# Cross attention over a long context: the key/value projection in pairs of 16-bit floats and 32-column matmuls

## The reference, cut to what matters

```python
q = x @ Wq.T                                   # x is layer-normalised
k_raw, v_raw = context @ Wk.T, context @ Wv.T
kv = concatenate([k_raw, v_raw], -1).reshape(b, m, 32, 8, 2)
k, v = kv[..., 0], kv[..., 1]                  # per head
q, k = rmsnorm(q), rmsnorm(k)                  # eps 1e-6
attn = softmax(q k^T * 8 ** -0.5)              # over 2048 context rows
x = x + attn @ v
```

## Time and profile before

| | before |
|---|---|
| median of 3 runs | 417.14 us (415.88 to 417.5) |
| span of the profiled execution | 413.8 us |
| PE busy | 388.5 us, 94% of the span |
| DVE, ACT, POOL busy | 303.8, 267.0, 208.3 us |
| L1790 matmuls (projection) | 192, busy 53.0 us |
| L1833 matmuls (values), L1820 (scores) | busy 69.7 and 25.9 us |
| L1741 (exponentials) | 128, busy 123.8 us |

### The profile page before, as it was taken

One profiled execution on the slowest core, in us unless ns is written; L12 is line 12 of the kernel. 1 busy time (PEld: TensorE's weight loads), 2 busy tenths in 40 slices (PEclk: granted clock), 3 DMA queues, 4 the chain that ended last, 5 costly groups with the idle time before them and its releaser, 6 DMA issues.

```text
span 413.8 us, 14357 instructions
## 1 busy us (share of the span) xinstructions
PE 388.5 (94%) x5999; PEld 322.5 (78%) x5999; DVE 303.8 (73%) x693; ACT 267.0 (65%) x553; POOL 208.3 (50%) x257
## 2 busy tenths in 40 slices
PE   6889989999999999889999999999889989999996
PEld 4567766777677777669999897778778878989995
DVE  7787989998688888758999996787997768222220
ACT  3588878887888888986454533823999136444441
POOL 2566677666566665106644440610498634445530
PEclk9999999999999999999999999999999999999999
DMA  5637731642321110380000017120000590000000
GB/s 162 230 117 245 232 123 52 195 141 73 85 65 39 30 29 6 114 320 2 2 2 1 2 44 306 39 103 2 2 0 3 176 388 2 2 1 2 0 2 25
DMA packets 10832, 34.78 MB, mean 84 GB/s; under 512 B 2192, under 2 KB 7312, under 8 KB 8976
## 3 DMA queue, kind: packets, MB, share of 16 engines
q1 hardware_dynamic: 10624, 33.86, 23.9%
q10 hardware_dynamic: 144, 0.00, 0.0%
HBM read 33.60 MB, written 0.26 MB: 82 GB/s over the span
## 4 chain that ended last, share of the span: by engine, by line
PE 59%; DVE 18%; POOL 9%; issue 8%; ACT 3%; DMA 1%; SPq 0%; DVEq 0%; POOLq 0%; ACTq 0%
PE ps L1833 10%; PE ps L1790 8%; PE ps L1244 8%; PE ps L1226 6%; PE ps L1820 4%; PE ps L1803 3%; PE ps L956 3%; PE ps L938 3%; PE ps L454 2%; PE ps L897 2%; POOL sb_halves L1632 2%; ACT sb_arena L1741 2%; PE ps L904 2%; DVE sb_big L635 2%; PE ps L1214 1%
## 5 line engine op out<-in xcount | busy, mean ns | idle before, releaser
L1741 ACT ACTIVATE sb_arena<-ps 128x1024 f32<-128x1024 f32 x128 | 123.8, 1020 | 19.2 <-PE ps L1820 18.3
L1833 PE MATMUL ps<-sb_arena 128*25 128x128 f32 (+1 forms) x2048 | 69.7, 274 | 1.9 <-issue 1.3
L1833 PEld LDWEIGHTS ps<-sb_arena 128*25 128x25 f32 (+1 forms) x2048 | 50.4, 97 | 10.0 <-issue 1.8
L1790 PE MATMUL ps<-sb_halves 128*128 128x512 f32 x192 | 53.0, 411 | 3.4 <-POOL sb_halves L1632 2.5
L1282 POOL TENSOR_TENSOR sb_halves<-sb_big,sb_halves 128x704 fp32r<-128x704 f32 x19 | 32.1, 1689 | 38.4 <-ACT sb_halves L1274 38.4
L1790 PEld LDWEIGHTS ps<-sb_halves 128*128 128x128 f32 x192 | 33.5, 188 | 16.0 <-issue 6.0
L1392 DVE SCALAR_TENSOR_TENSOR sb_arena<-ps,sb_w_q,sb_arena 128x176 f32<-128x176 f32 x40 | 15.9, 401 | 40.3 <-ACT sb_arena L1300 40.0
L1244 PE MATMUL ps<-sb_halves 128*128 128x352 f32 x240 | 43.7, 333 | 1.8 <-DVE sb_halves L1345 1.0
L544 POOL TENSOR_TENSOR sb_halves<-sb_big,sb_halves 128x256 fp32r<-128x256 f32 x28 | 21.6, 793 | 44.3 <-ACT sb_halves L528 44.3
L1623 POOL TENSOR_TENSOR sb_big<-sb_arena 128x256 f32<-128x256 f32 x30 | 18.7, 624 | 47.0 <-DVE sb_arena L1500 47.0
L1244 PEld LDWEIGHTS ps<-sb_halves 128*128 128x128 f32 x240 | 39.0, 189 | 3.6 <-issue 2.4
(11 more groups left out here) (249 smaller groups left out, 850.6 us busy)
## 6 DMA issues: line engine op xcount, KB each, us to landing
sb_arena<-in_ctx SPq DMA_DIRECT2D x32, 128.0 KB, 2.8
sb_mid<-in_w_down SPq DMA_DIRECT2D x1, 3584.0 KB, 11.7
sb_big<-in_w_gu SPq DMA_DIRECT2D x1, 3520.0 KB, 11.8
sb_mid<-in_w_ffn SPq DMA_DIRECT2D x3, 768.0 KB, 4.5
sb_big<-in_w_gu SPq DMA_DIRECT2D x1, 2112.0 KB, 8.0
sb_big<-in_w_q SPq DMA_DIRECT2D x2, 1024.0 KB, 5.1
sb_big<-in_w_k SPq DMA_DIRECT2D x2, 1024.0 KB, 6.3
sb_big<-in_w_v SPq DMA_DIRECT2D x2, 1024.0 KB, 5.7
```

What stands on the lines that cost most here:

```text
L1741: nc.scalar.activation(probs[:, n % P_SLOTS].rearrange("p a g n -> p a (g n)"), ps[:, bank:bank + 2], ACT.Exp, scale=XD ** -0.5).then_inc( ...
L1790: i = T.matmul(ps[:, 7], ctx_half[:, t % 2, c, kt], wkv_half[:, d, kt], start=(n + kt == 0), stop=(n == 2 and kt == KT - 1))
L1833: i = T.matmul(ps[32 * gg:32 * gg + m, 6, j * P:(j + 1) * P], v_sb[:, t % V_SLOTS, 4 * gg + j, head], probs[:, n % P_SLOTS, a, gg], start= ...
```

## The change

Context and weights are still split into a high and a low part, but the parts are 16-bit floats (F16). The key/value weights are multiplied by 256 when they are split (on ScalarE by an activation with a scale in place of a copy, on VectorE by a scalar_tensor_tensor in place of a tensor_tensor); the ones that count the softmax's denominator become 256, and the epsilon of the keys' norm is multiplied by 256 squared. The pairs lie in a part of `w_ri` that is not yet loaded then, no longer in `halves`. In `project`, each of the six matmuls of 128 columns becomes four of 32 columns that write 32 partitions each of the same bank, 24 in all. The order of the steps on every engine and all waits stay as they are; the lines of the kernel below L1552 move down by one to four (the matmul L1790 becomes L1794).

```diff
-        wkv_half = halves[:, 0:2048].rearrange("p (c k n) -> p c k n", c=2, k=KT)
-        ctx_half = halves[:, 2048:3072].rearrange("p (s c k m) -> p s c k m", s=2, c=2, k=KT)
+        x_pairs = w_ri[:].rearrange("p c t n -> p (c t n)")
+        wkv_half = x_pairs[:, 1024:2048].bitcast(F16).rearrange("p (c k n) -> p c k n", c=2, k=KT)
+        ctx_half = x_pairs[:, 2048:2560].bitcast(F16).rearrange("p (s c k m) -> p s c k m", s=2, c=2, k=KT)
...
-            V.memset(v_sb[:, :, :, 8:9], 1.0)
-            V.memset(v_sb[:, :, :, 33:34], 1.0)
+            V.memset(v_sb[:, :, :, 8:9], W_SCALE)
+            V.memset(v_sb[:, :, :, 33:34], W_SCALE)
...
-            V.tensor_tensor(wkv_half[:, 1], w_xkv, wkv_half[:, 0].bitcast(F32), ALU.subtract).then_inc(sem("wkv_split"), 1)
+            V.scalar_tensor_tensor(wkv_half[:, 1], w_xkv, W_SCALE, wkv_half[:, 0], ALU.mult, ALU.subtract
+                                   ).then_inc(sem("wkv_split"), 1)
...
-                G.tensor_tensor(ctx_half[:, t % 2, 1], ctxT[:, t % CTX_SLOTS], ctx_half[:, t % 2, 0].bitcast(F32),
+                G.tensor_tensor(ctx_half[:, t % 2, 1], ctxT[:, t % CTX_SLOTS], ctx_half[:, t % 2, 0],
                                 ALU.subtract).then_inc(sem("ctx_split"), 1)
...
-            nc.scalar.copy(wkv_half[:, 0], w_xkv).then_inc(sem("wkv_high"), 1)
+            nc.scalar.activation(wkv_half[:, 0], w_xkv, ACT.Copy, scale=W_SCALE).then_inc(sem("wkv_high"), 1)
...
-                nc.scalar.activation(kln, kms[:, t % 2], ACT.Ln, bias=1e-6, scale=1.0 / XD).then_inc(sem("k_log"), 1)
+                nc.scalar.activation(kln, kms[:, t % 2], ACT.Ln, bias=1e-6 * W_SCALE ** 2, scale=1.0 / XD).then_inc(sem("k_log"), 1)
...
                     for kt in range(KT):
-                        i = T.matmul(ps[:, 7], ctx_half[:, t % 2, c, kt], wkv_half[:, d, kt], start=(n + kt == 0),
-                                     stop=(n == 2 and kt == KT - 1))
+                        for r in range(0, P, 32):
+                            i = T.matmul(ps[r:r + 32, 7], ctx_half[:, t % 2, c, kt, r:r + 32], wkv_half[:, d, kt],
+                                         start=(n + kt == 0), stop=(n == 2 and kt == KT - 1), skip_group_check=True)
```

More of the change, by code:

```diff
@@ L52 @@
 TURN_AT = 13
+W_SCALE = 256.0
 LATE_GU = slice(4 * 2 * EI, E * 2 * EI)
```

## The result

After the change the kernel takes 425.7 us (median of 4 runs, 422.9 to 428.3) against 417.3 before: a ratio of 1.021, 95% interval 1.018 to 1.024. I had forecast 414.0 and a range up to 416.8. It is slower, by 8.4 us, where I had forecast some 3 less.

What follows compares the result with a forecast made beforehand. VectorE and GpSimd's loop (4.69 to 4.81 us) was taken to bind, practically tied with TensorE's 4.71. Gains of 0.8 + 0.3 + 0.8 + 0.8 + 0.4 = 3.1 off the span of 413.8, plus 3.3, gave 414.0 us, range 409.5 to 416.8.

Steps and rivals of the forecast that it cites:

- The projection: Key/value projection on TensorE: 24 matmuls of 32 columns take 1.49 us instead of 1.66, 0.17 less a round.
- the early switch: On TensorE, from values to projection: the projection starts 0.18 before the values' end instead of 0.07, 0.11 less a round.
- TensorE's own round: Cross attention, one projection to the next on TensorE: from 4.71 to 4.43 us, 0.28 less.
- less overlap: Rival on the projection's four column groups: 0.28 a group, 24 matmuls in 1.79, no gain, 416.5 to 417.5 us; chance 0.13.
- two pairs: Rival on the projection: only two column groups run at a time, projection 2.6 us, kernel 439 us; chance 0.04.
- The loop of VectorE and GpSimd: Cross attention: the two engines wait on each other in a closed loop, 4.69 us a round, 4.81 in the first half.
- GpSimd's split: Context split on GpSimd, now writing 16 bits: no change taken, bounds -0.1 and +0.08 us a round.
- TensorE really binds: Rival in the cross attention: TensorE sets the round, so its whole saving counts, 8.2 us, 408.9 us; chance 0.10.
- rounds of 4.4: Sign in the cross attention: rounds falling to 4.4 us would prove the prediction wrong, TensorE binding after all.
- More halts for instructions: Rival on TensorE's queue: one more halt of 1.11 us gives 415.1, three 417; chance 0.08, shared with a slower cast.
- The single stretches of the sum: Gains by part of the cross attention: 0.8 + 0.3 + 0.8 + 0.8 + 0.4 = 3.1 us off the span.
- The frame: Step from profiled span to measured time: the median lies 3.3 us above the span, 410.7 becoming 414.0.

Runs made afterwards that it cites:

- e1_wide: The changed kernel with the projection as six 16-bit matmuls of 128 columns instead of 24 of 32: 412.6 us, 0.990 of the kernel before.
- e9_light_pool: e1_wide with GpSimd's two weighing steps on 8 columns instead of 128, most of the weighted sum left out: 414.5 us, 0.997 of the kernel before.
- e4_wide_turn: The changed kernel with keys turned by 8 transposes of 128 columns instead of 32 of 32: 410.4 us, 0.985 of the kernel before.
- e5_held_loads: The changed kernel with later parts' weights loaded together after the last context tile: time not compared; last values end at 179.0 us, 11.7 earlier.
- e2_waits: The kernel before the change with 1152 already fulfilled waits added to TensorE's queue: 460.8 us, 1.103 of the kernel before.

## Why the prediction was wrong

**The projection: right.** The 24 matmuls take 1.48 against 1.49, the early switch is 0.18, and TensorE's own round is 4.41 against 4.43. The rivals with less overlap and with two pairs, at 1.79 and 2.6, are out. The Trainium skill, "TensorE: Matmul & The Clock Gate", section "Measured speedup vs the span model", gives 3.07 times for four row tiles with 512 moved. Carried over to four column groups, as the prediction did, that meant an estimated 0.29 a group; the trace does not agree, with 24 matmuls in 1.48.

**The loop of VectorE and GpSimd: right, and a little shorter.** Where no halts disturb it, the second half goes at 4.62 and the first at 4.75, against 4.69 and 4.81. Most of the difference is GpSimd's split, for which I took no change with -0.1 as a bound. The view by line has it (20 to 178 us, count | busy us, mean ns | idle):

```profile
L1635 POOL TENSOR_TENSOR sb_w_ri<-sb_arena,sb_w_ri 128x256 f16<-128x256 f32 x28 | 18.8, 673 | 2.2
...
L1633 POOL CAST sb_w_ri<-sb_arena 128x256 f16<-128x256 f32 x28 | 12.4, 444 | 0.0
```

The subtraction takes 673 against 728, the cast 444 against 443. VectorE's L1522 stood still until GpSimd's step was through in e1_wide (0.69, its end 0.29 after L1646's), and no longer when GpSimd's steps became short in e9_light_pool (0.43). The Trainium skill, "SBUF — State Buffer", section "Who interferes with whom", says that VectorE and GpSimd share a pair of ports as an exclusive lock; the trace agrees. "TensorE really binds" is out too: in e1_wide, with TensorE 0.24 early, the round stays at 4.62. The prediction named rounds of 4.4 as a sign against it. In the changed kernel three rounds of 4.41 occur; the one at 82.89 follows a halt of 0.74, behind which TensorE was late, so I don't count them as that sign.

**"More halts for instructions": the step that failed.** I had the right event, the right count (576 matmuls and as many loads) and the wrong price. I left the term out of the sum and kept it as a rival: I read the halt at 173.75 as an accident of 1.11 us that might come once or three times more, 415.1 or 417. It was the visible end of a supply that runs throughout: a block of 256 instructions every 4.54 us, fetched in 3.4 to 4.4. The term should have been a rate. 310 instructions in 4.41 us are 70 per us, against 274 in 4.71, 58. That is a fifth more per us, because there are more instructions and because the round is shorter, and the block often falls below the time that its successor needs. In the profiled execution the size was 16.6 us of halts and an estimated 3.4 of clock, in place of 1 to 3; in the medians the time came out 8.4 longer instead of 3 shorter.

The Trainium skill, "Runtime: NRT & Kernel Launch", section "Instruction fetch mechanics", says that instructions come in blocks of 16 KiB, 256 of them, and that the cost of crossing from one to the next is mostly hidden. The trace agrees with the blocks; with 20.5 us of halts the cost is not hidden here.

**The sum.** Where the added halts are absent, the time lies in the stated range and below the forecast: e1_wide (412.6, without the early switch) and e4_wide_turn (410.4, with it) come out 1.4 and 3.6 below 414.0. The shorter split, some 28 x 0.06, is an estimated 1.7 of it, and e4_wide_turn has 3.2 us less of halts than the kernel before (0.7 against 3.9). The single stretches of the sum I did not check one by one.

**The frame.** I took 3.3 us to lie outside the span. In every run of which both are listed it is 1.5 to 1.8. By that the profiled execution of before took an estimated 415.5 us, below the lowest of its runs: the rest was that it was a quick one, and so the forecast set a quick span beside a median.

## What to carry to other kernels

Count what an engine's queue uses up per us, waits included, and look for halts "issue" that lie a fixed number of instructions apart. If such halts are there already, more and smaller instructions can cost more than they save. Then it can pay to take instructions away elsewhere on the same engine: here 24 transposes a round, with their weight loads, turned 2% lost into 1.5% gained, while the same edit in the kernel before gained nothing. Large loads that are issued just before a block of instructions is fetched can delay it, so their place in the round counts. An experiment that adds instructions should use such as cost little by themselves: here waits did not.

## What the runs showed of the hardware

- TensorE's queue gets its instructions, weight loads and waits counted, in blocks of 256. In the changed kernel, between 30 and 165 us, a packet took 0.9 to 1.6 us, and the first of its instructions started no less than 1.2 us after it had landed.
- Behind a weight load such a packet started up to 3.9 us after the block ahead had begun (at most 2.3 in e5_held_loads, without those loads).
- In the changed kernel TensorE's granted clock was 0.50 for 3.4 us twice, each time soon after TensorE had stood still for 2.01 us.
- A wait in TensorE's queue that is already fulfilled takes 51 ns in the trace of e2_waits, and is not hidden: with 1152 of them the kernel took 44 us longer.
- Two unused weight loads of 32 columns beside each matmul of 512 moved lengthened the 24 matmuls by about 0.1 us in the chain of waits (1.37 to 1.44 against 1.29).
